# Layer 0 of a graph network on one NeuronCore: scaled rows are added into 5 DRAM copies of the aggregate by accumulating indirect DMA, instead of being moved to their window and summed there

## What is computed

```
row = concat(src, 0..N-1); col = concat(dst, 0..N-1); w = concat(edge_weight, 1)
deg = segment_sum(w, row);  dinv = deg ** -0.5 (0 where deg is 0)
agg = segment_sum(dinv[row] * w * dinv[col] * x[col], row)      # over 400,000 edges + N loops
x   = layernorm(x + agg @ W.T + b)
# then layer 1: a message per edge from x[src], x[dst] and an attribute, summed by dst, and a GRU step
```

## Time and profile before

| | us |
|---|---|
| median of 3 runs | 13771.09 |
| lowest, highest | 13733.34, 13771.17 |
| the profiled execution's span | 13922.2 |
| of it `counts` | 1329 |
| `move_rows` | 5094 |
| `sum_moved` | 1094 |
| `nodes` | 298 |
| `messages` | 5595 |

### The profile page before, as it was taken

The page is one execution under the profiler, slowest core; times in us unless marked ns, Lnnn a source line. Parts: engine busy times, 40 slices in busy tenths (PEclk is TensorE's granted clock), DMA queues, the critical chain, the costliest instruction groups (busy, mean ns, idle before and its releaser), DMA issues. The chain is left out here.

```text
span 13922.2 us, 224925 instructions
## 1 busy us (share of the span) xinstructions
PE 7333.5 (53%) x59154; PEld 5652.1 (41%) x59155; DVE 6189.5 (44%) x18214; ACT 2164.2 (16%) x7321; POOL 7524.3 (54%) x7666
## 2 busy tenths in 40 slices
PE   5777444444444444444666654555555555555558
PEld 4666222222222222222555443444444444444555
DVE  7999422222222222222899633333333333333333
ACT  0000011111111111111677200000000000000001
POOL 3666566656655555565555055555555555555552
PEclk9999766666666666666555566666666666666665
DMA  7200122112111112121344222222222222222221
GB/s 279 112 0 0 50 61 62 60 61 61 60 61 61 60 61 61 60 60 58 108 110 111 53 78 78 77 77 75 74 77 75 74 76 74 72 71 71 73 71 35
DMA packets 591229, 1008.48 MB, mean 72 GB/s; under 512 B 180946, under 2 KB 304943, under 8 KB 590943
## 3 DMA queue, kind: packets, MB, share of 16 engines
q1 hardware_dynamic: 391196, 698.88, 16.4%
q0 software_dynamic: 200000, 309.20, 8.0%
HBM read 759.90 MB, written 247.61 MB: 72 GB/s over the span
## 5 line engine op out<-in xcount | busy, mean ns | idle before, releaser
L1138 POOL DMA_INDIRECT a_rows<-a_half,src_i x3125 | 2957.8, 947 | 2935.9 <-ACT src_i L1223 2086.3
L782 POOL DMA_INDIRECT moved<-rows,place x3125 | 3048.7, 976 | 2106.6 <-issue 999.9
L690 DVE CUSTOM_DVE_ANT_0 junk<-ps_place,place_hot 128x98 f32<-128x98 f32 x3125 | 610.9, 255 | 3354.6 <-remote 2802.1
L1271 PE MATMUL ps_pre<-tables,m_dst_hot 128*128 x10830 | 1145.5, 280 | 1604.7 <-DVE m_dst_hot L1196 1361.7
L1271 PEld LDWEIGHTS ps_pre<-tables,m_dst_hot 128*128 128x128 bf16 x10830 | 950.0, 128 | 1834.3 <-issue 1803.5
L1243 PE MATMUL ps_msum<-src_cols,node_hot 128*128 128x129 f32 x7220 | 1511.6, 373 | 342.9 <-issue 300.9
L1161 DVE TENSOR_TENSOR src_cols<-ps_pre,a_rows 128x640 f32<-128x640 f32 x625 | 515.8, 825 | 2358.8 <-remote 1944.4
L1243 PEld LDWEIGHTS ps_msum<-src_cols,node_hot 128*128 128x128 f32 x7220 | 1351.9, 278 | 386.0 <-issue 333.3
L751 PE MATMUL ps_place<-place_hot,upto_bf 128*128 128x490 bf16 x624 | 339.3, 544 | 2072.4 <-DVE place_f L690 1874.0
L772 ACT ACTIVATE rows<-ps_rows,edge_cols 128x64 f32<-128x64 f32 x3125 | 706.4, 322 | 4376.5 <-remote 3002.9
L1233 ACT ACTIVATE src_cols<-src_cols 128x640 f32<-128x640 f32 x625 | 461.0, 738 | 5071.9 <-DVE src_cols L1161 4812.8
(11 more groups left out here) (211 smaller groups left out, 10317.8 us busy)
## 6 DMA issues: line engine op xcount, KB each, us to landing
dst_rows<-in_dst SPq DMA_DIRECT2D x625, 320.0 KB
m_dst_rows<-in_dst SPq DMA_DIRECT2D x625, 320.0 KB
tables<-moved SPq DMA_DIRECT2D x723, 162.5 KB, 2.2
moved<-sums SPq DMA_DIRECT2D x180, 650.0 KB, 14.3
moved<-rows,place POOLq DMA_INDIRECT x3125
a_rows<-a_half,src_i POOLq DMA_INDIRECT x3125
attr_rows<-attr_parts SPq DMA_DIRECT2D x625, 11.2 KB
attr_parts<-tables SPq DMA_DIRECT2D x9, 781.2 KB, 8.0
```

What stands on the lines that cost most here:

```text
L782: pool.indirect_dma_start(out=moved[:, :], out_offset=bass.IndirectOffsetOnAxis(ap=place[:, s, j:j + 1], axis=0), in_=rows[:, s, j, :], in ...
L1138: pool.indirect_dma_start(out=a_rows[:, s, j, :], out_offset=None, in_=a_dram[:, :], in_offset=bass.IndirectOffsetOnAxis(ap=src_i[:, s, j: ...
L1271: last = pe.matmul(ps_pre[:, h, j * HD:(j + 1) * HD], dst_hot[:, slot, j * P:(j + 1) * P], cols(tables, win * (3 * HD) + i * HD, HD), star ...
```

## The change

`counts` becomes `degrees`: without the window counts, `start_row` and `q_tab`; it clears 5 DRAM arrays `aggs[j]` (`AROWS` = 12,672 rows of 64 floats each) and makes `src_f`, the `src` numbers as floats. `move_rows` becomes `scatter_rows`: no places from running counts; a row goes straight to its node's row of the copy `aggs[j]`, j being the tile's number in its group, by an indirect DMA that adds. Nodes that repeat within a tile are summed first: DVE compares each edge's `src` with the 128 of its tile (`same`), and 5 f32 products (L683) give every edge the sum over its equals; all but the first of equals go to a row that nobody reads (`trash`). The DMAs of tiles 0 to 2 of a group wait for those of the group before (`landed_early`), and those of tiles 3 and 4 for theirs (`landed_late`). `sum_moved` becomes `sum_copies`: 5 loads and 4 additions. `nodes` and `messages` only keep some tiles elsewhere (`a_out` in `src_f`, `a_rows` in `weight`).

```diff
-def move_rows(nc, dst, lane_row, node_id, before_bf, upto_bf, ones_bf, ones, zero_bf, src_hi, src_lo, weight,
-              step_tab, start_row, tables, moved):
+def scatter_rows(nc, src, dst, lane_row, node_id, ones_bf, earlier, trash, src_hi, src_lo, src_f, weight,
+                 step_tab, tables, aggs):
...
@@ SP
-                wait(sp, placed, g - (S - 1))
-                sp.dma_start(dst_rows[:, s, :], dst[bass.ds(g * GE, GE)].unsqueeze(0).to_broadcast([P, GE])).then_inc(rows_in[s], 16)
+                wait(sp, gathered, g - 1)
+                wait(sp, same_made, g - 1)
+                h = s % 2
+                for ids, of in ((dst_rows, dst), (src_rows, src)):
+                    sp.dma_start(ids[:, h, :], of[bass.ds(g * GE, GE)].unsqueeze(0).to_broadcast([P, GE])).then_inc(rows_in[s], 16)
@@ DVE, after dst_hot
-                if not is_first(g):
-                    read_places(*last_of(g, s, use))
-
-                dve.tensor_tensor(hi_hot[:, s % 2, :, :], lane_row[:, 0:NW].unsqueeze(1).to_broadcast([P, G, NW]),
-                                  cols(src_hi, g * G, G).unsqueeze(2).to_broadcast([P, G, NW]), ALU.is_equal).then_inc(hi_made, 1)
+                wait(dve, totalled, g - 1)
+                dve.tensor_tensor(same[:, h, :, :], split3(src_rows[:, h, :], G),
+                                  cols(src_f, g * G, G).unsqueeze(2).to_broadcast([P, G, P]), ALU.is_equal).then_inc(same_made, 1)
+                dve.scalar_tensor_tensor(home[:, h, :], cols(src_lo, g * G, G), float(NW), cols(src_hi, g * G, G),
+                                         ALU.mult, ALU.add).then_inc(homes, 1)
+                dve.wait_ge(same_made, g + 1)
+                for j in range(G):
+                    last = dve.tensor_tensor_reduce(junk[:, j, :], same[:, h, j, :], earlier[:, :], 1.0, 0.0,
+                                                    ALU.mult, ALU.add, repeats[:, h, j:j + 1])
...
+                wait(dve, landed_late, (g - (S - 1)) * (16 * (G - EARLY)))
+                wait(dve, landed_early, (g - (S - 1)) * (16 * EARLY))
+                dve.tensor_tensor(place[:, s, :], moved_to[:, h, :], home[:, h, :], ALU.max).then_inc(placed, 1)
@@ PE
+            def add_up(g, h):
+                pe.wait_ge(scaled, g + 1)
+                pe.wait_ge(same_made, g + 1)
+
+                wait(pe, kept, g - 1)
+                for j in range(G):
+                    last = pe.matmul(ps_total[:, h, j * D:(j + 1) * D], same[:, h, j, :], rows[:, h, j * D:(j + 1) * D], start=True, stop=True)
+                last.then_inc(totalled, 1)
@@ ACT
+            def keep(g, s):
+                act.wait_ge(totalled, g + 1)
...
+                act.activation(total[:, s, :], ps_total[:, s % 2, 0:G * D], ACT.Copy).then_inc(kept, 1)
@@ POOL
-                pool.wait_ge(cast, g + 1)
-                wait_alone(pool, rows_ready, g + 1, passed)
+                pool.wait_ge(placed, g + 1)
+                wait_alone(pool, kept, g + 1, passed)
+                if not is_first(g):
+                    wait_alone(pool, landed_early, g * (16 * EARLY), passed)
                 for j in range(G):
-                    pool.indirect_dma_start(out=moved[:, :], out_offset=bass.IndirectOffsetOnAxis(ap=place[:, s, j:j + 1], axis=0),
-                                            in_=rows[:, s, j, :], in_offset=None).then_inc(scattered[s], 16)
+                    if j == EARLY and not is_first(g):
+                        wait_alone(pool, landed_late, g * (16 * (G - EARLY)), passed)
+                    pool.indirect_dma_start(out=aggs[j][:, :], out_offset=bass.IndirectOffsetOnAxis(ap=place[:, s, j:j + 1], axis=0),
+                                            in_=total[:, s, j * D:(j + 1) * D], in_offset=None, compute_op=ALU.add).then_inc(landed_early if j < EARLY else landed_late, 16)
...
-def sum_moved(nc, lane_row, ones, q_tab, tables, moved, acc):
+def sum_copies(nc, tables, aggs, acc):
...
+        flat = tables[:, :].bitcast(F32)
+        copies = [acc] + [flat[:, (i % 3) * NW * D:(i % 3 + 1) * NW * D] for i in range(G - 1)]
...
+            for i in range(G):
+                wait(sp, added, i - 3)
+                sp.dma_start(copies[i], aggs[i][0:NW * P, :].rearrange("(p a) c -> p (a c)", p=P)).then_inc(copy_in[i], 16)
...
+            dve.wait_ge(copy_in[0], 16)
+            for i in range(1, G):
+                dve.wait_ge(copy_in[i], 16)
+                wait(dve, added, i - 1)
+                dve.tensor_tensor(acc, acc, copies[i], ALU.add).then_inc(added, 1)
```

More of the change, by code:

```diff
@@ L337, in _, with steps_table @@
             over_pairs(act, NB, copy)
-def steps_table(nc, dst, before, table, sums, step_tab, q_tab):
+def steps_table(nc, dst, before, table, sums, step_tab):
     R = NG // G
@@ L450, in _, with degrees @@
             split_bf16(dve, then, wide[:, 0, :], wide[:, 1, :], [parts[:, i, :] for i in range(3)], attr_done)
-def counts(nc, lane_row, ident, ones_bf, before, tables, src_hi, src_lo, weight, moved, places, sums, dinv, start_row, q_tab, attr_in_parts):
-    ZG = 4
+def degrees(nc, lane_row, tables, src_hi, src_lo, src_f, weight, aggs, sums, dinv, attr_in_parts):
     with ExitStack() as ctx:
@@ L495, in _ @@
             sp.wait_ge(zeroed, 1)
[L496 to L507, removed]
+            for agg in aggs:
+                sp.dma_start(agg.rearrange("(p r) c -> p (r c)", p=P), zeros).then_inc(zero_done, 16)
+            sp.wait_ge(zero_done, 16 * G)
             sp.wait_ge(attr_in_parts, 16 * 9)
@@ L753, in body @@
                 if not is_first(g):
[L755 to L762 removed]
+                    add_up(g - 1, 1 - h)
@@ L774, in _ @@
+                last.then_inc(scaled, 1)
+                if not is_first(g):
+                    keep(g - 1, (s - 1) % S)
             over_groups(act, NG, body)
+            keep(NG - 1, (NG - 1) % S)
         @block.gpsimd
@@ L908, in _ @@
-            over_groups(dve, NQ, body, load, slots=SL)
-            wins = load(NQ - LAG, LAG)
-            for i in range(LAG):
-                add(NQ - LAG + i, (NQ - LAG + i) % SL, wins[LAG + i])
-        @block.tensor
-        def _(pe):
-            def body(q, s, use, _):
-                pe.wait_ge(hot_made, q + 1)
-                pe.wait_ge(act_hot_made, q + 1)
-                wait(pe, added, q - (SL - 1))
-                for j in range(G):
-                    parts = high_rows(s)[:, j, :], high_halves(left[:, s, :])[:, j * D:(j + 1) * D], rest[:, s, j * D:(j + 1) * D]
-                    for i, part in enumerate(parts):
-                        last = pe.matmul(ps[:, s, 0:D], hot[:, s, j, :], part, start=(i == j == 0), stop=(i == 2 and j == G - 1))
-                last.then_inc(summed, 1)
-            over_groups(pe, NQ, body, slots=SL)
```

256 lines of the change are left out of this document (69 added, 187 removed).

## The result

| | before | after |
|---|---|---|
| median of 10 runs each, us | 13,755.0 | 13,791.5 |
| lowest, highest | 13,733.3, 13,771.3 | 13,774.1, 13,803.8 |
| ratio, 95% interval | | 1.0021 (1.0013 to 1.0029) |
| profiled span | 13,922.2 | 13,796.9 |

The forecast of 13,150 us was wrong. The time lies in the range, but not on the side that it named. The first runs of the experiments add a fact that the table doesn't show: on another chip the same two kernels take 11,345 and 12,217 us, and there the change is 7.7% slower.

The account below looks back on a forecast made before the run. The prediction took POOL's DMA issues plus pauses, 8.15 us a group, to bound the scatter stage. 13922 - 1035 (summing stage, degrees) + 406 (scatter) = 13293 us, scaled to 13,150; range 11,800 to 14,450.

Parts of the forecast that it names:

- I take the row's 0.976 us: Scatter stage, POOL: an adding DMA's issue costs the same 0.976 us as a plain one, five a group.
- rival C: Scatter stage: slower by POOL's issue, at 1.4 us each 14,450 us; decides at 1.18 us an issue; chance 0.14.
- What the pause becomes: Scatter stage: POOL's pause grows 2.1 us to 6.2, giving 8.8 us a group, 5500 us, +406 us.
- The 1.1% between profiled run and median: Whole kernel: profiled execution is 1.1% above the runs' median, so 13,293 us is scaled by 0.989 to 13,150.
- the gain side: Summing stage and degrees: replacing the 1094 us summing stage gains 1029 us, degrees 6; together -1035 us.
- Landings: Scatter stage: POOL's waits for landings of the group before cost nothing, taken as 0.
- The estimate of 2.1 us: Scatter stage: landing time for 32 KB, about 2.0 us plus bytes over 436 GB/s, meaning no wait.
- Rival A: Scatter stage: PE no longer starves, POOL's issues alone set 6.7 us a group; 11,850 us; chance 0.23.
- Rival B: Scatter stage: slower by landings, at L = 9 us 11.55 us a group, 14,850 us; chance 0.13.

Follow-up runs that it names:

- e9: Changed kernel with an overwriting scatter of only the first 64 rows per DMA; scatter stage 5104 us, on a chip where the kernel before takes 13,787 us.
- e10: Kernel before with 5 empty POOL instructions behind each indirect DMA of move_rows and messages; 11,603 us, beside 11,365 for the kernel before.
- e11: Kernel before with 12 empty POOL instructions behind each indirect DMA of both stages; 13,076 us, beside 11,365 for the kernel before.
- e2: Kernel before with the scatter of move_rows turned into an adding one; 13,185 us against 11,361, ratio 1.160.
- e1: Changed kernel with a scatter that overwrites instead of adding; 10,477 us against 11,361 for the kernel before, ratio 0.922.
- e5: Kernel before, unchanged, run and profiled on another chip; 11,345 us.
- e4: Changed kernel, each group's first adding DMA waiting for all five landings of the group before; 13,457 us.
- e7: Changed kernel, each adding DMA taking only the first 64 of its 128 rows; 11,877 us.
- e3: Changed kernel, adding only the first 32 of the 64 floats of each row; 12,190 us, against 12,217 with whole rows.
- e8: Changed kernel with an overwriting scatter, run once more; 10,472 us beside 11,345 for the kernel before.
- e17: Kernel before with an adding scatter in move_rows, run once more; 13,180 us, beside 11,352 to 11,390 for the kernel before.

## Why the prediction was wrong

- **The step that failed: "I take the row's 0.976 us".** The issue of an adding DMA is 1.59 us on average. I had an estimate of 1.46 for the case that each row needs a third description, and rival C's 1.18 as the point of decision, and took the lower bound, as it was "the same list of 128 rows". It cost 5 x 0.61 = 3.07 us a group, 1919 us.
- **The second, in the other direction: "What the pause becomes".** I added 2.1 us to a pause that went away. Of the predicted 8.8 us, 6.38 were issues and 2.42 pauses; measured were 9.45 and 0.19. The two errors are +3.07 and -2.23 us, +0.84 a group, +525 us for the stage. The reading behind it, that PE starves while POOL issues and is released 2 us after the last issue, was right for plain DMAs on such a chip (e9 repeats it) and wrong as a rule for any issuing: under adding ones, which keep POOL busier, PE runs freely. It was also wrong in that DVE and ACT wait for PE: they are held themselves, so the chain that I lengthened by PE's products and ACT's copy began later than I had it. PE's ten f32 passes took 2.38 us (1486.3 / 625) and not 1.8, at a mean granted clock of 0.50 (the 2.34 us of the earlier trace rows, read as 1.2 GHz, lie in a stretch for which the profile gives a clock of 1.00); this is hidden behind POOL.
- **The 1.1% between profiled run and median** isn't a property of both kernels. 13,293 x 0.989 gave 13,150; after has a factor of 0.9996. That is 140 of the 641 us by which I missed, the stage 525, and the small terms -24.
- **Right: the gain side.** `sum_copies` took 52 us (65 forecast, 35 to 95), since its loads land 7.4 us apart and hide all additions but the last; `degrees` and the turn behind it gained 9 us (6 forecast); `messages` kept its time. Landings cost 0.16 us a group (0 forecast). A plain DMA of 128 rows lands in 2.5 us in the middle in e10 and 2.3 in e11, an adding one in 3.2 (e2). The estimate of 2.1 us from the Trainium skill's page "DMA: Bandwidth & Descriptors", section "Anatomy of one DMA — SWDGE (gpsimd) path", is near the plain ones and too low for the adding one.
- **Rival A** is what e1 shows: 6.87 us a group for 6.7 forecast, but on a chip that doesn't starve PE. The old list starves on one chip and not on another (e5), and the new one starves in e9. The Trainium skill's page "Runtime: NRT & Kernel Launch", section "Instruction fetch mechanics", says that a taken branch breaks the prefetch of instructions; as the cause of the starving it would have gone by PE's own list, and these runs don't bear that out.
- **Rival B** decides at L = 7.3 us; L is 3.2 to 3.95 (e2, e4).
- **Rival C had the mechanism, and I put its point of decision wrong.** 1.18 us an issue supposed that the pauses stay. Without them the stage breaks even at 8.15 + 1.66 = 9.8 us a group, (9.8 - 0.19) / 5 - 0.30 = 1.62 us an issue, and 1.59 is just below: hence the tie. On a chip that doesn't starve PE the point is 6.63 + 1.66 = 8.3 us a group or 1.32 us an issue, and the change loses (9.67 - 6.63) x 625 = 1900 us against a gain of 1040. The difference, 860 us, is that of the two times there (872).

So the tie is chance. The new stage costs some 1900 us more than the old one where PE isn't starved (6048 - 4144), 1752 of them by adding (6048 - 4296, e1); on the recorded chip, 950 (5094 - 4144) fall where the old kernel's POOL stood idle because PE, DVE and ACT were starved, and the remaining 934 are nearly as much as the summing stage was worth. That last step, that adding ends the starving there, rests on comparing the recorded traces with e9; adding in the old kernel couldn't be seen on such a chip. By these rates the kernel before, scatter and summing together, costs 6.63 + 1.75 = 8.4 us a group where PE isn't starved and 8.15 + 1.75 = 9.9 where it is, and the changed one 9.7 on both. The 0.2 us between 9.9 and 9.7 are less than the 160 us by which before's profiled run is long, and in the runs before is 0.2% ahead. So the change pays on neither kind of chip seen here.

## What to carry to other kernels

Before an operation takes the place of one that "looks the same" to its queue, price its issue by itself when the engine that issues it is near the bound; here one measured adding DMA would have put 9.45 us in the place of 6.38, above the 8.15 of the whole group before, and left only the question of what the pauses do. A pause whose cause the profile can't name isn't a term to carry over: it may vanish with the change or on another chip, so work the sum out with and without it. When an engine's wait has no named releaser, look up when the work that it needs had ended: here that was 8 to 10 us before, which says that the engine didn't wait for it. And compare stages, not totals, when one kernel is measured on two chips.

## What was unexpected of the hardware

- An adding indirect DMA of 128 rows takes POOL 1.553 us to issue, a plain one 0.958; by row 2.2 against 1.0 ns (e7 and e9, two sizes each), by byte nothing (e3), so the larger part of the difference is a fixed 0.44 us. It lands in 3.2 us (e2), a plain one in 2.3 to 2.5 (e11, e10).
- Two states, by chip or by time: where plain indirect DMAs are issued 1.2 to 1.3 us apart, PE, DVE and ACT are starved in some runs (the recorded ones and e9) and not in others (e1 to e8 and e10 to e17, on five chips). For the kernel before this is 13,755 against 11,345 us, 21%; stages without indirect DMAs are equal to within 0.3%.
- POOL's issues 1.86 us apart that add don't starve PE on the recorded chip, although POOL is busy 82% of that stage.
